# A transposing maximum that writes f16, and two small transpositions as f16 products, in a fused attention and expert layer

## The chip, the cores and the metric

The kernel runs on one core of one Trainium2 chip. The metric is device time in microseconds (us), the median of a few executions, lower is better.

## What is computed

A batch of 16 sequences of 1024 tokens, 256 wide, goes through two sublayers, each as `x = x + layernorm(f(layernorm(x)))`. The first is attention with 16 heads of 16 and relative positions:

```python
qk = einsum('bhld,bhrd->bhlr', q, k) / sqrt(16)
qk = qk + einsum('bhld,lrd->bhlr', q, rel)      # rel[l, r] = rel_emb[r - l + 511]
att = softmax(qk, axis=-1)
out = einsum('bhlr,bhrd->bhld', att, v)
```

The second is a dense product plus a shared and six routed low-rank experts, of which each token takes two.

## The kernel before

The work is 128 tiles (`NT`) of 128 queries. A tile is 16 groups (`NG`), numbered g; g = 4*jp + k, where jp is one of four pairs of 128-key chunks and k one of four sets of 32 queries (`IW`). So there are 2048 groups. Each group's scores lie in two PSUM banks (one for each chunk c of the pair) as keys on the rows and (head, query) on the columns, 16 x 32 = 512 columns a bank; three such pairs of banks (`NBUF`) go round.

For the softmax a maximum over the 256 keys of the pair is subtracted from each (head, query). Keys lie on the rows, so it is found in steps. On VectorE, `maxima` (L957) transposes 32 x 32 blocks and reduces over 32 keys: L960 writes `r1`, 128 rows x 32 columns, of which 16 belong to each chunk. On TensorE, `transpose_max` (L669) brings both halves of `r1` with two transpositions (L672) to 16 rows (heads) x 256 columns in the PSUM tile `p_max`. On VectorE, `spread` (L963) takes the maximum over the eight blocks with the sign turned (L969), writes it as f16 to `nm` (16 heads x 2 x 128 queries), and multiplies it with a mask into `nmm` (L972). On TensorE, `shift` (L681) adds `nmm` to the scores with 16 products whose stationary operand `pick` is 128 x 128 f16. Then ScalarE takes the exponential (L845), and in the next four groups TensorE multiplies `prob` with the values (L691, 32 columns of the array for each head, four heads side by side), and ScalarE copies the result out. At k=1 the product of L725 transposes the `nm` of the pair before to 128 queries x 16 heads, from which the parts of the four pairs are later rescaled against one another.

The order is written out by hand for every engine. TensorE does in group g: the scores of chunk 0 (L660 x8, 64 columns, and L665 x16, 32 columns, both with 96 rows), `transpose_max` of group g-1 (behind a wait for its maximum), the scores of chunk 1 (again L660 and L665), then `wide` and `mixed`, and at the end `shift` of group g-1. `wide` holds at k=1 and k=2 the value products L691, at k=3 four transpositions L698, at k=0 parts of the projection of a later tile (L703, L712). `mixed` holds L725 at k=1 and, in certain groups, products of the output projection and the second sublayer (L703, L712, L747). Ahead of `mixed`, and at k=2 and k=3 of `wide` as well, TensorE waits for L969 of group g-1. VectorE does in group g: `spread` of g-1, `maxima` of g, and then the `side` work of that group for layer norms, gates and rescaling (`dm` at g=1, `gate` and `ceq` at g=5, `yn` at g=13, `y2n` at g=14 among them). GpSimd masks the queries into `qm` and `rm` (L532, L533), splits f32 values into two f16 parts and does sums in f32 (`wp`, `osum`, `qkb`). In a tile it does, behind the statistics of g=13, the sum into `x1`, the masks of the next tile, and from there on the splits of that tile's start.

The unit matrices are `ident` (128 x 128, f32) and `ident16` (16 x 16, f16); GpSimd makes them once ahead of the loops.

Of the kernel before, what the change touches and what calls it, by code (L numbers as in the profile page):

```python
# [9 lines left out]
H, HD = 16, 16  # L10
# [3 lines left out]
P = 128  # L14
# [4 lines left out]
IW = 32  # L19
# [19 lines left out]
def sandwich_kernel(nc, x, wqT, bq, wkT, bk, wvT, bv, woT, bo, relT, baseT, base_b,  # L39
                    shAT, shBT, roAT, roBT, rtT, rtb, out):  # L40
    f32, f16 = mybir.dt.float32, mybir.dt.float16
    ALU = mybir.AluOpType
# [10 lines left out]
    with ctx:  # L53
        def sb(name, shape, dt=f32):
            return ctx.enter_context(nc.sbuf_tensor(name, shape, dt))
# [3 lines left out]


        ident = sb("ident", [P, P])
        ident16 = sb("ident16", [H, H], f16)
        pick = sb("pick", [P, H // 2, P], f16)
        mask_h = sb("mask_h", [H, 2, IW], f16)
        mask_q = sb("mask_q", [ROWS, H, IW], f16)
# [34 lines left out]
        qm = sb("qm", [ROWS, NI, H, IW], f16)  # L100
        rm = sb("rm", [ROWS, NI, IW // 2, H, 2], f16)
        prob = sb("prob", [P, 2, 2, H, P])
        r1 = sb("r1", [P, 2 * H])
        nm = sb("nm", [H, 2, P], f16)
        nmm = sb("nmm", [P, 2, IW], f16)
        ot = sb("ot", [P, 4, P])
        parts = sb("parts", [P, NJP, H, 17])
# [77 lines left out]
        p_max = pm[0:H, 0:2 * P]  # L185
        p_n = pm[:, 2 * P:3 * P]
# [303 lines left out]
        def _(pool):  # L490
            g = nc.gpsimd
# [9 lines left out]
            g.memset(one[:, :], 1.0)  # L501
            g.memset(vpad[:, :, :], 1.0)
            g.memset(nmm[:, :, :], 0.0)
            pool.drain()

            def keep(v, op, base, pattern, mult):
                g.affine_select(out=v, in_=v, compare_op=op, fill=0.0, base=base, pattern=pattern,
                                channel_multiplier=mult)

            keep(ident[:, :], ALU.is_equal, 0, [[-1, P]], 1)  # L510
            keep(ident16[:, :], ALU.is_equal, 0, [[-1, H]], 1)
            half_h = H // 2
            for h0 in (0, half_h):
                g.affine_select(out=pick[:, :, :], in_=pick[:, :, :], compare_op=ALU.not_equal, fill=1.0,
# [132 lines left out]
        def _(pe):  # L647
            mm = nc.tensor.matmul
# [20 lines left out]
            def transpose_max(g_count):  # L669
                pe.wait_ge(s_rmax, g_count)  # L670
                for c in range(2):
                    last = nc.tensor.transpose(p_max[:, c * P:(c + 1) * P], r1[:, c * H:(c + 1) * H], ident[:, :])  # L672
                last.then_inc(s_maxT, 1)

            def shift(buf, g_count):
# [25 lines left out]
            def transpose2(dst, src):  # L701
                for c in range(2):
                    last = nc.tensor.transpose(dst[:, c * P:(c + 1) * P], src[:, c * P:(c + 1) * P],  # L703
                                               ident[:, :])
                return last

            def product(dst, *pairs):


                steps = [(lhs(i), rhs(j)) for lhs, rhs in pairs for i, j in ((0, 0), (0, 1), (1, 0))]  # L710
                for m, (lhs, rhs) in enumerate(steps):
                    last = mm(dst, lhs, rhs, start=(m == 0), stop=(m == len(steps) - 1))  # L712
                return last

            def both(lhs, rhs, cols=slice(None)):

                return [(lambda i, c=c: lhs[:, i, c, cols], lambda j, c=c: rhs[:, j, c, :]) for c in range(2)]

            def mixed(t, g, att, a, b):


                jp, k = divmod(g, NI)
                if k == 1 and (a if jp == 0 else att):

                    mm(p_n[:, 0:H], nm[:, (jp - 1) % 2, :], ident16[:, :], start=True, stop=True)\  # L725
                        .then_inc(s_nmtp, 1)
                    return s_nmt, t * NJP + jp
                if g == 0 and b:
                    pe.wait_ge(s_xn1, t - 1)
                    transpose2(p_t, xn1).then_inc(s_x1Tp, 1)  # L730
                    return s_x1T, t - 1
                if g == 3 and b:

                    pe.wait_ge(s_x1T2, t - 1)
                    product(p_t[:, 0:NH], *both(x1T2, w_a2)).then_inc(s_hp, 1)
                    return s_hf, t - 1
                if g == 8 and a:
                    pe.wait_ge(s_o, t)
                    transpose2(p_t, o[:, :, :].rearrange("p h d -> p (h d)")).then_inc(s_oTp, 1)
                    return s_oT, t  # L740
                if g == 11 and a:
                    pe.wait_ge(s_oT2, t)
                    product(p_t, *both(oT2, w_o2)).then_inc(s_wo, 1)
                    return s_y0, t
                if g == 10 and b:
                    pe.wait_ge(s_hw, t - 1)
                    nc.tensor.transpose(p_n[0:NA, :], hw[:, :], ident[:, :]).then_inc(s_hTp, 1)  # L747
                    return s_hT, t - 1
                if g == 12 and b:
                    pe.wait_ge(s_hT2, t - 1)  # L750
                    product(p_t, *both(x1T2, w_base2), (lambda i: hT2[:, i, :], lambda j: w_b2[:, j, :]))\
                        .then_inc(s_y2p, 1)
                    return s_y20, t - 1
                return None
# [39 lines left out]
            def tile(t, n, att, proj, a, b, ph=None):  # L794
                read = None
                for g in range(NG):
                    jp, k = divmod(g, NI)
                    old = a if g == 0 else att
                    if att:
                        if k == 0:  # L800
                            pe.wait_ge(s_tw[jp], t * 16 + 16)
                            pe.wait_ge(s_ks[jp], batch_of(t) * 96 + 96)
                        if jp == 0:
                            pe.wait_ge(s_mask, t * NI + k + 1)
                        free = t * NG + g - NBUF + 1
                        if not (isinstance(free, int) and free <= 0):
                            pe.wait_ge(s_exp, free)
                        scores(g, 0, buffer(ph, g))
                    if read is not None:
                        pe.wait_ge(*read)  # L810
                    if old:
                        transpose_max(t * NG + g)
                    if att:
                        scores(g, 1, buffer(ph, g)).then_inc(s_scores, 1)

                    wide_first = k == 1 or g in (0, 8)
                    if wide_first:
                        wide(t, n, g, att, proj, a)
                    if old:
                        pe.wait_ge(s_nmr, t * NG + g)  # L820
                    read = mixed(t, g, att, a, b)
                    if not wide_first:
                        wide(t, n, g, att, proj, a)
                    if old:
                        shift(buffer(ph, g - 1), t * NG + g)
# [92 lines left out]
        def _(dve):  # L918
# [44 lines left out]
            def spread(g, count):  # L963


                jp, i = divmod(g, NI)
                dve.wait_ge(s_maxT, count)
                part = nm[:, jp % 2, i * IW:(i + 1) * IW]
                v.tensor_reduce(part, p_max.rearrange("h (q i) -> h i q", i=IW), axis=AX.X, op=ALU.max,  # L969
                                negate=True).then_inc(s_nmr, 1)  # L970
                dve.drain()  # L971
                v.tensor_tensor(nmm[0:H, :, :], part.rearrange("h (a i) -> h a i", a=1)  # L972
                                .to_broadcast((H, 2, IW)), mask_h[:, :, :], ALU.mult).then_inc(s_nm, 1)
# [90 lines left out]
            def tile(t, n, att, proj, a, b, ph=None):  # L1064
                for g in range(NG):

                    if a if g == 0 else att:
                        spread((g - 1) % NG, t * NG + g)
                    if att:
                        maxima(buffer(ph, g), t * NG + g + 1)  # L1070
                    side(g, t, n, proj, a, b)
# [35 lines left out]
```

## Time and profile before

| | us |
|---|---|
| median of 3 runs | 6519.43 (6518.75 to 6520.47) |
| profiled execution, its own time | 6501.09 |
| its span | 6499.3 |
| TensorE products busy | 6203.9 (95%) |
| VectorE busy | 5036.1 (77%) |
| GpSimd busy | 3640.9 (56%) |
| ScalarE busy | 3134.0 (48%) |

The granted clock of TensorE over the span is 0.99 of full speed, 2.4 GHz. PE are products of TensorE, PEld its weight loads, which run beside products; DVE is VectorE, ACT ScalarE, POOL GpSimd, SP the engine that issues the transfers. In a row, `128*16` after the operands are the rows and columns of the stationary operand, and then stand the shapes of the moving operand's reading or the output. A product lasts longer than the distance to the next one, since products overlap: distances are to be read from starts. A row `x16` on the timeline starts with its first instruction and ends with its last. "Idle before" is the engine's pause before the row, and behind it who ended it.

### The profile page before, as it was taken

How to read it: one execution, taken by the hardware profiler on the slowest of the kernel's cores; microseconds unless marked ns; L12 is line 12 of the kernel's file. 1: busy time of each engine (PE TensorE's matmuls, PEld its weight loads, DVE VectorE, ACT ScalarE, POOL GpSimd, SP SyncE). 2: the span in 40 equal slices, each digit the busy share in tenths (PEclk: the TensorE clock that was granted, in tenths of full speed). 3: DMA queues.
4: the chain of work that ended last, by engine and by line, in shares of the span. 5: the costliest groups of instructions: out<-in, count | busy, mean ns of one | idle time of the engine just before them, and what ended most of it. 6: DMA issues, size and time to landing. Idle time of an engine off the chain costs nothing.

```text
span 6499.3 us, 408509 instructions
## 1 busy us (share of the span) xinstructions
PE 6203.9 (95%) x178176; PEld 5783.0 (89%) x178176; DVE 5036.1 (77%) x10289; ACT 3134.0 (48%) x5145; POOL 3640.9 (56%) x4707
## 2 busy tenths in 40 slices
PE   5999999999999999999999999999999999999997
PEld 4999899999999999999999999899999999998997
DVE  3777777777787777777777777777777777777776
ACT  2444444444444444444444444444444444444444
POOL 5555555555565555555555555555555555555555
PEclk8999999999999999999999999999999999999998
DMA  3111121111212112121111211112111121211210
GB/s 86 37 44 50 37 58 37 51 45 35 58 36 59 35 35 61 35 60 33 42 56 35 60 36 48 45 39 58 35 52 43 35 58 38 59 35 33 62 35 27
DMA packets 570089, 296.73 MB, mean 46 GB/s; under 512 B 384176, under 2 KB 534688, under 8 KB 568624
## 3 DMA queue, kind: packets, MB, share of 16 engines
q1 hardware_dynamic: 568624, 272.86, 15.2%
q8 instruction: 1450, 23.76, 1.5%
q14 instruction: 15, 0.12, 0.0%
HBM read 184.46 MB, written 88.60 MB: 42 GB/s over the span
## 4 chain that ended last, share of the span: by engine, by line
PE 75%; DVE 15%; issue 6%; DVEq 3%; POOLq 1%; POOL 0%; SPq 0%; ACT 0%; DMA 0%
PE sc L665 19%; PE sc L681 13%; PE sc L660 11%; PE pw L691 11%; DVE r L960 6%; PE pm L672 6%; PE pm L712 4%; PE pw L698 4%; PE pw L712 4%; DVE nm L969 3%; DVE ceq L1008 2%; DVEq L971 2%; DVE y2n L926 1%; DVE dm L983 1%; PE pm L703 1%
## 5 line engine op out<-in xcount | busy, mean ns | idle before, releaser
L960 DVE TRANSPOSE_TENSOR_REDUCE r<-sc 128x32 f32<-128x1024 f32 x2048 | 2547.5, 1244 | 49.2 <-PE sc L665 48.3
L665 PE MATMUL sc<-rm,tw 96*128 96x32 f16 x65536 | 2288.9, 176 | 58.1 <-issue 58.1
L845 ACT ACTIVATE prob<-sc 128x1024 f32<-128x1024 f32 x2048 | 2095.7, 1023 | 237.9 <-PE sc L681 173.7
L665 PEld LDWEIGHTS sc<-rm,tw 96*128 96x128 f16 x65536 | 1976.9, 97 | 64.7 <-issue 64.3
L660 PE MATMUL sc<-qm,ks 96*128 96x64 f16 x32768 | 1635.2, 193 | 29.9 <-DMA ks<-qk_s 15.1
L969 DVE TENSOR_REDUCE nm<-pm 16x32 f16<-16x256 f32 x2048 | 840.5, 410 | 932.2 <-PE pm L672 931.4
L660 PEld LDWEIGHTS sc<-qm,ks 96*128 96x128 f16 x32768 | 1380.8, 98 | 105.7 <-issue 35.2
L681 PE MATMUL sc<-nmm,pick 128*128 128x64 f16 x32768 | 1305.7, 194 | 1.4 <-DVE nmm L972 1.4
L681 PEld LDWEIGHTS sc<-nmm,pick 128*128 128x128 f16 x32768 | 1150.9, 98 | 126.9 <-issue 103.2
L691 PE MATMUL pw<-prob,vs 128*32 128x128 f32 x32768 | 1110.2, 276 | 100.2 <-DVE nm L969 89.9
L691 PEld LDWEIGHTS pw<-prob,vs 128*32 128x32 f32 x32768 | 835.2, 110 | 158.5 <-DVE nm L969 119.8
L972 DVE TENSOR_TENSOR nmm<-nm,mask_h 16x64 f16<-16x64 f16 x2048 | 697.5, 341 | 195.0 <-issue 9.8
L672 PE MATMUL pm<-ident,r 128*16 128x128 f32 x4096 | 777.8, 271 | 0.6 <-DVE r L960 0.5
L837 ACT ACTIVATE ot<-pw 128x512 f32<-128x512 f32 x512 | 305.7, 597 | 741.4 <-PE pw L691 741.4
L545 POOL TENSOR_TENSOR oT<-oT,one 128x256 f16<-128x256 f32 x128 | 78.3, 612 | 967.4 <-ACT oT L837 967.4
L533 POOL TENSOR_TENSOR rm<-raw,mask_r 96x512 f16<-96x512 f16 x515 | 607.5, 1180 | 0.0
L532 POOL TENSOR_TENSOR qm<-raw,mask_q 96x512 f16<-96x512 f16 x515 | 590.1, 1146 | 20.7 <-PE sc L665 11.2
L837 ACT ACTIVATE nmt<-pm 128x16 f32<-128x16 f32 x512 | 94.0, 184 | 800.3 <-PE pm L725 800.3
L578 POOL TENSOR_TENSOR wp<-parts,wst 128x1088 f32<-128x1088 f32 x128 | 275.5, 2152 | 166.5 <-ACT parts L837 166.5
L837 ACT ACTIVATE parts<-pw 128x272 f32<-128x272 f32 x512 | 203.3, 397 | 315.5 <-PE pw L698 308.7
L698 PE MATMUL pw<-ident,ot 128*128 128x128 f32 x2048 | 322.9, 280 | 14.3 <-DVE nm L969 6.6
L541 POOL TENSOR_TENSOR rs<-ve,mhalf 128x1 f32<-128x1 f32 x521 | 286.3, 550 | 74.0
(129 smaller groups left out, 5753.9 us busy)
## 6 DMA issues: line engine op xcount, KB each, us to landing
raw<-qk_s SPq DMA_DIRECT2D x774, 64.0 KB, 2.5
tw<-tw_s SPq DMA_DIRECT2D x512, 72.0 KB, 2.0
v_s<-vpad SPq DMA_DIRECT2D x136, 256.0 KB, 3.4
vs<-v_s SPq DMA_DIRECT2D x64, 512.0 KB, 3.7
ks<-qk_s SPq DMA_DIRECT2D x384, 64.0 KB, 2.4
xin<-x SPq DMA_DIRECT2D x138, 128.0 KB, 2.1
qk_s<-qkh SPq DMA_DIRECT2D x272, 64.0 KB, 1.7
qk_s<-qkl SPq DMA_DIRECT2D x272, 64.0 KB, 1.6
```

Source lines behind the costliest of these rows:

```text
L532: g.tensor_tensor(qm[:, i, :, :], src, mask_q[:, :, :], ALU.mult)
L533: g.tensor_tensor(rm[:, i, :, :, :].rearrange("p i h s -> p h i s"), src.rearrange("p h (i s) -> p h i s", s=2), mask_r[:, :, :].rearrange ...
L660: last = mm(bank[:, 2 * h * IW:(2 * h + 2) * IW], ks[:, h, j:j + P], qm[:, i, 2 * h:2 * h + 2, :].rearrange("p h i -> p (h i)"), start=(h ...
L665: last = mm(out3[:, :, 2 * k:2 * k + 2], tw[:, jp, u:u + P], rm[:, i, k, :, :], start=False, stop=False, skip_group_check=True)
L672: last = nc.tensor.transpose(p_max[:, c * P:(c + 1) * P], r1[:, c * H:(c + 1) * H], ident[:, :])
L681: last = mm(pairs[:, :, h, :], pick[:, h, :], nmm[:, :, :], start=False, stop=True, skip_group_check=True)
L691: last = mm(pw[32 * q:32 * q + 32, col * P:(col + 1) * P], vs[:, 2 * jp + c, h, :], prob[:, jp % 2, c, h, :], start=(c == 0), stop=(c == 1))
L837: return A(dst, src, ACT.Copy)
L845: A(prob[:, jp % 2, :, :, i * IW:(i + 1) * IW], sc[:, 2 * buf:2 * buf + 2, :].rearrange("p c (h i) -> p c h i", i=IW), ACT.Exp).then_inc(s ...
L960: v.tensor_reduce(r1[:, :], sc[:, 2 * buf:2 * buf + 2, :].rearrange("p c (h i) -> p (c h) i", i=IW), axis=AX.X, op=ALU.max, apply_transpos ...
L969: v.tensor_reduce(part, p_max.rearrange("h (q i) -> h i q", i=IW), axis=AX.X, op=ALU.max, negate=True).then_inc(s_nmr, 1)
L972: v.tensor_tensor(nmm[0:H, :, :], part.rearrange("h (a i) -> h a i", a=1) .to_broadcast((H, 2, IW)), mask_h[:, :, :], ALU.mult).then_inc(s ...
```

## The change

`r1` becomes f16, so L960 writes its maxima as f16. The two transpositions of L672 become ordinary products of `r1` (f16, 128 x 16) with `ident16` (f16, now 128 x 128). `nm` gets 128 rows; rows 16 to 127 are set to zero once and stay so, and VectorE writes rows 0 to 15 as before. The product of L725 reads all 128 rows of `nm` and 16 columns of `ident16`.

```diff
-        ident16 = sb("ident16", [H, H], f16)
+        ident16 = sb("ident16", [P, P], f16)
...
-        r1 = sb("r1", [P, 2 * H])
-        nm = sb("nm", [H, 2, P], f16)
+        r1 = sb("r1", [P, 2 * H], f16)
+        nm = sb("nm", [P, 2, P], f16)
...
             g.memset(nmm[:, :, :], 0.0)
+            g.memset(nm[:, :, :], 0.0)
             pool.drain()
...
-            keep(ident16[:, :], ALU.is_equal, 0, [[-1, H]], 1)
+            keep(ident16[:, :], ALU.is_equal, 0, [[-1, P]], 1)
...
                 for c in range(2):
-                    last = nc.tensor.transpose(p_max[:, c * P:(c + 1) * P], r1[:, c * H:(c + 1) * H], ident[:, :])
+                    last = mm(p_max[:, c * P:(c + 1) * P], r1[:, c * H:(c + 1) * H], ident16[:, :], start=True, stop=True)
                 last.then_inc(s_maxT, 1)
...
-                    mm(p_n[:, 0:H], nm[:, (jp - 1) % 2, :], ident16[:, :], start=True, stop=True)\
+                    mm(p_n[:, 0:H], nm[:, (jp - 1) % 2, :], ident16[:, 0:H], start=True, stop=True)\
                         .then_inc(s_nmtp, 1)
...
-                part = nm[:, jp % 2, i * IW:(i + 1) * IW]
+                part = nm[0:H, jp % 2, i * IW:(i + 1) * IW]
```

## Rows read from the trace of the kernel before

**Rows 1.** The page of the kernel before: engines (part 1) and the chain (part 4).

```profile
PE 6203.9 (95%) x178176; PEld 5783.0 (89%) x178176; DVE 5036.1 (77%) x10289; ACT 3134.0 (48%) x5145; POOL 3640.9 (56%) x4707
...
PE 75%; DVE 15%; issue 6%; DVEq 3%; POOLq 1%; POOL 0%; SPq 0%; ACT 0%; DMA 0%
```

**Rows 2.** Waits of all engines: who waited for whom: us in total, times, longest.

```profile
DVE nm L969 <- PE pm L672: 931.4, 1551, 1.8
...
PEld pw L691 <- DVE nm L969: 119.8, 210, 0.8
...
PEld pw L698 <- DVE nm L969: 26.6, 126, 0.3
```

**Rows 3.** Groups by form, columns as in the page's part 5.

```profile
L960 DVE TRANSPOSE_TENSOR_REDUCE r<-sc 128x32 f32<-128x1024 f32 x2048 | 2547.5, 1244 | 49.2 <-PE sc L665 48.3 <-issue 0.3
...
L672 PE MATMUL pm<-ident,r 128*16 128x128 f32 x4096 | 777.8, 271 | 0.6 <-DVE r L960 0.5
...
L712 PE MATMUL pw<-xT,w_q 128*128 128x128 f16 x1632 | 119.7, 225 | 30.3 <-POOL xT L547 29.1 <-DVE nm L969 1.2
...
L725 PE MATMUL pm<-ident,nm 16*128 16x16 f16 x512 | 91.0, 178 | 0.0
```

**Rows 4.** Timeline of PE in one group: start us, us, what, count, idle before.

```profile
3055.85 0.56 PE L665 MATMUL sc<-rm,tw 96*128 96x32 f16 x16
3056.25 0.38 PE L672 MATMUL pm<-ident,r 128*16 128x128 f32 x2
3056.47 0.40 PE L660 MATMUL sc<-qm,ks 96*128 96x64 f16 x8
```

**Rows 5.** Timeline of PE, then of its weight loads, around L691 and L725.

```profile
3062.01 0.56 PE L665 MATMUL sc<-rm,tw 96*128 96x32 f16 x16
3062.50 1.08 PE L691 MATMUL pw<-prob,vs 128*32 128x128 f32 x32
3063.51 0.18 PE L725 MATMUL pm<-ident,nm 16*128 16x16 f16 x1
3063.62 0.64 PE L681 MATMUL sc<-nmm,pick 128*128 128x64 f16 x16
...
3063.51 0.09 PEld L725 LDWEIGHTS pm<-ident,nm 16*128 16x128 f16 x1 [0.20 <-issue]
3063.62 0.52 PEld L681 LDWEIGHTS sc<-nmm,pick 128*128 128x128 f16 x16
```

**Rows 6.** Timeline of PE: the two sets of twelve f16 products in g=4.

```profile
3095.59 0.84 PE L712 MATMUL pw<-xT,w_q 128*128 128x128 f16 x12
3096.27 0.83 PE L712 MATMUL pw<-xT,w_k 128*128 128x128 f16 x12
```

**Rows 7.** Timeline of all engines from g=5 to g=6 of one tile.

```profile
3098.78 1.04 POOL L592 TENSOR_TENSOR qkb<-qkf,b_qk 128x512 f32<-128x512 f32 x1
3098.97 0.89 DVE L972 TENSOR_TENSOR nmm<-nm,mask_h 16x64 f16<-16x64 f16 x1
...
3101.45 1.00 DVE L1008 TENSOR_TENSOR ceq<-gate 128x36 f32<-128x36 f32 x1
...
3102.93 0.54 PE L691 MATMUL pw<-prob,vs 128*32 128x128 f32 x12 [0.70 <-DVE nm L969]
```

**Rows 8.** Timeline of all engines around g=15 and around g=2 of the next tile.

```profile
3080.43 0.69 DVE L926 TENSOR_SCALAR y2n<-y,mv,rs 128x256 f32<-128x256 f32 x1
...
3081.50 0.66 PE L698 MATMUL pw<-ident,ot 128*128 128x128 f32 x4 [0.17 <-DVE nm L969]
...
3088.20 1.15 POOL L533 TENSOR_TENSOR rm<-raw,mask_r 96x512 f16<-96x512 f16 x1
...
3088.55 0.88 DVE L983 TENSOR_TENSOR dm<-nmin,nmt 128x64 f32<-128x64 f32 x1
...
3089.15 0.56 PE L665 MATMUL sc<-rm,tw 96*128 96x32 f16 x16
...
3089.82 0.43 PE L691 MATMUL pw<-prob,vs 128*32 128x128 f32 x8
```

## The prediction

> **What bounds the kernel now.** I read the engine table and the chain first, then the waits, then single groups of 32 queries on the timeline. TensorE is busy 95% of the span and holds 75% of the chain that ended last, VectorE 15% [rows 1]. The waits say where that 15% is: VectorE waits for the transpositions of L672 in 1551 of 2048 groups, so it usually has time left; the other way round, TensorE waits for `nm` (L969) about 210 times before the value products of L691 and 126 times before L698 [rows 2]. With 128 tiles of 16 groups that is three groups of a tile, and the timeline shows which: g=6 and g=15 of every tile and g=2 of most [rows 7, 8]. Everywhere else a nanosecond of TensorE is a nanosecond of the kernel.
>
> **Part 1: two f32 transpositions become two f16 products.** On the timeline one group runs L660 x8, L665 x16, L672 x2, L660 x8 with no idle time. From the start of L665 to the next L660 is 0.62 us; fifteen of the sixteen L665 steps take 15 x 25 ns = 0.375 us (0.40 us for 16), so from the last L665 to the L660 behind the transpositions is 0.245 us: 25 ns, then 110 ns for each transposition [rows 4]. An f16 product with 128 moving columns takes 0.68 us / 12 = 56 ns [rows 6]. Taken alone, that saves 54 ns twice, 0.11 us a group.
>
> But the row has a second property. The stationary operand of L672 is 128*16, and the new L672 is an ordinary product with it. Two ordinary products of the kernel use a part of the array, L691 (128*32) and L725 (16*128), and both pay when they begin and end [rows 5]: L665 to L691 is 0.49 us where L665 to L672 is 0.40, so entering costs 0.085 us (0.11 from the last L665 instead of 0.025); L725, with 16 moving columns, holds the next product back 0.11 us where the L681 behind it go 0.48/16 = 30 ns apart; and the weight loads of L725 and L681 begin in the same hundredth as their products, with 0.20 us of idle loader before L725: they are not pulled ahead. The f32 transposition of today, also 128*16, shows none of this: it comes 25 ns behind L665 and L660 comes 110 ns behind it, just its own length [rows 4]. So the row allows two readings: the narrow operand is placed on the whole array only because it is a transposition, or 16 columns never narrow the array. I take the first: L725, with only 16 rows, is an ordinary product and behaves as a narrowed one, and so does L691, with 32 columns; the new L672 is of their kind, and its 16 columns are not padded.
>
> The price under that reading: 0.11 to enter, 0.056 between the two, and to leave 0.11 (L725's) plus 112 more columns at 56/128 ns, about 0.155. Sum 0.32 us against 0.245: **0.075 us a group more, not 0.11 less.** Bounds for the leaving: 0.11 (L725 as it stands), giving +0.03, and 0.22 (the last round of L691, L691's block of 1.01 us being eight rounds), giving +0.14. I take 0.155 because the width of the moving operand is the one difference to L725. The end of the second product comes 0.11+0.056+0.225 = 0.39 us after the last L665, against 0.025+0.11+0.27 = 0.405 [rows 3, 4], so `spread` on VectorE starts practically as now; only the second half of the scores, and with it the next maxima, starts later.
>
> The Trainium skill bears on this in TensorEngine Tiling, Key Properties: changing the tiling mode drains TensorE; its Restrictions say column tiling rules out the f32 transpose mode. The first agrees with L691 and L725, the second with the absence of any gap at today's L672. Against that, the same skill's TensorE: Matmul & The Clock Gate, section "Wait — 56ns, not 53.3ns?", gives 56 ns between f16 products of 128 columns; by that alone the group would save 0.11 us, which is the first rival.
>
> **Part 2: `nm` padded to 128 rows.** L725 then takes the whole array, as L681 behind it. What it still pays is the change from L691, which L681 pays in its place at k=2. Behind it L681 follows after 25 to 30 ns instead of 110: 0.085 us less, 512 times. The lower bound is nothing (if the 0.11 were the product itself), the upper 0.085. The second memset and the larger unit matrix cost fractions of a microsecond once, ahead of the loop. VectorE writes rows 0 to 15 as before.
>
> **Part 3: the maximum writes f16.** L960 reads 1024 f32 a row from PSUM in 1244 ns and writes 32 values [rows 3]; 16-bit output of so few values I cost at nothing; no row shows this form. Bounds: 30 ns either way (the spread between its 1.23 and 1.25 us pieces doubled). It lies on the path only in three groups of a tile, so at most 3 x 128 x 0.03 = 12 us.
>
> **What is absorbed.** In front of g=6, TensorE waits 0.70 us for a stretch that VectorE and GpSimd set: `nmm` of g=5 takes 0.89 us instead of 0.18, ending with GpSimd's `qkb` (98.78+1.04), then the maxima, then `ceq` 1.00 us [rows 7]. GpSimd's run up to `qkb` started with the parts of g=3. So what TensorE loses or gains in g=4, 5 and 6, and L725 of g=5, disappears in that wait. Likewise `y2n` of g=14 (0.69 us) sets g=15, where TensorE waits 0.17, and `dm` (0.88), which ends with GpSimd's `rm` (88.20+1.15), sets g=2: there L665 to L691 is 0.67 us instead of 0.49, 0.18 us of waiting [rows 8]. In the code GpSimd writes all masks behind the statistics of g=13 in one row, so I take its run from there to g=2 as fixed, and g=14, 15, 0, 1, 2 together with L725 of g=13 and g=1 cost 5 x 0.075 - 2 x 0.085 = 0.2 us, less than the 0.35 us of waits. There remain eight groups (3 and 7 to 13) and L725 of g=9: 8 x 0.075 - 0.085 = 0.515 us a tile, x 128 = **66 us more**. The profiled execution took 6501.1 us, its span 6499.3, so it would be 6567; the median of the runs shown is 18 us above the profiled one, and 6519.4 + 66 = **6585 us**. With nothing absorbed it is 2048 x 0.075 - 512 x 0.085 = 110 us, 6630; with leaving at its lower bound, 8 x 0.03 - 0.085 = 0.155 us a tile, 6539.
>
> **Rivals.**
> First, faster: no change of the array's shape, the product goes at 56 ns. Each group then saves 0.11 and the same eight groups and one L725 count, the waits of g=2, 6 and 15 growing by what is lost: 8 x 0.11 + 0.085 = 0.965 us a tile, 123 us, 6396 us. For it: today's L672 is 128*16 and pays nothing. Against it: L725 is just as small and pays. It decides if L660 follows the second product within 0.06 us. It could give more: `nmm` of g=5 reaches VectorE only 0.19 us after `qkb` has begun [rows 7], and 0.2 us earlier it would slip in ahead of it, taking most of the 0.70 us wait with it. With every group and all L725 counted, 16 x 0.11 + 4 x 0.085 = 2.1 us a tile, it is 269 us, 6250 us.
>
> Second, no change: leaving costs as little as L725's 0.11 and more of it is absorbed in the waits than I count, or the saved 0.085 at L725 counts in all four groups: 8 x 0.03 - 4 x 0.085 is -0.1 us a tile, 13 us less, 6506 us.
>
> Third, slower than I say: leaving at 0.22, nothing absorbed, 2048 x 0.14 - 43 = 244 us, 6763 us. L691's rounds are f32 and run at half the f16 rate, so I give this little.
>
> That the f16 maximum is something other than the f32 maximum rounded is not visible in a time; `nm` is f16 already.
>
> **How the numbers follow.** The forecast has 0.70, the first rival 0.20, the second 0.08, the third 0.02. The forecast's own range is 6535 to 6640. One case in five is faster, and leaving it all out would leave no room for anything else, so the range goes down to that rival's nearer end: 6395 to 6640. About 0.2%, 13 us, is what a measurement of this kernel can tell from no change. Slower by more than that: the forecast but for its lowest edge, and the third, 0.70; same, 0.09; faster, 0.21.
>
> **What would show it.** Under the forecast L672 (f16, two products) has a mean near 225 ns, but the L665 ahead of it and the L660 behind it are 0.32 us apart, and a loader row of L672 and of L660 shows idle time or starts with its product, as L725's does now; TensorE's busy time falls while the span grows; the 0.70 us before L691 in g=6 shrinks to about 0.5. L725 to L681 is 30 ns. VectorE's total wait for L672 changes little. I am wrong if L660 starts within 60 ns of the second L672: then the first rival holds and the waits on `nm` grow. I am wrong about the absorption if the waits before L691 and L698 are as long as now. I am wrong about part 2 if L681 still comes 110 ns behind L725.

## The result and the profile after

The changed kernel takes 6637.26 us (median of 4 runs, 6616.80 to 6639.35) against 6519.56 us, 1.0173 times the kernel before, 95% interval 1.0153 to 1.0194: slower. The medians differ by 118 us; 1.0173 is 113 us, since one of the four runs is 20 us faster than the others and counts fully in the ratio. The profiled execution took 6616.8 us, 116 us more than that of before. The diff adds lines, so L672 is now L673, L660 and L665 are L661 and L666, L691 is L692, L698 is L699, L712 is L713, L725 is L726, and L969 is L970.

First the page: span, engines, and the chain.

```profile
span 6615.0 us, 408510 instructions
...
PE 6310.2 (95%) x178176; PEld 5679.0 (86%) x178176; DVE 5147.6 (78%) x10289; ACT 3137.3 (47%) x5145; POOL 3639.0 (55%) x4708
...
PE 86%; DVE 7%; issue 5%; DVEq 1%; POOLq 1%; POOL 0%; SPq 0%; ACT 0%; DMA 0%
PE sc L666 22%; PE sc L661 16%; PE pw L692 15%; PE sc L682 14%; PE pm L673 6%; PE pw L713 4%; PE pm L713 3%; PE pw L699 3%; DVE xn L927 3%; DVE r L961 2%; PE pm L704 1%; PE pm L726 1%; DVEq L972 1%; DVE nm L970 1%; DVE ceq L1009 1%
```

Against [rows 1], products are busy for 106 us more, although each L673 got shorter, and the chain has moved from VectorE (15% to 7%) to TensorE (75% to 86%). Then one group on TensorE's timeline (start, length in us, what, count), and the weight loads of the same stretch:

```profile
3066.24 0.56 PE L666 MATMUL sc<-rm,tw 96*128 96x32 f16 x16
3066.73 0.28 PE L673 MATMUL pm<-ident,r 128*16 128x128 f16 x2
3066.94 0.41 PE L661 MATMUL sc<-qm,ks 96*128 96x64 f16 x8
```

```profile
3066.73 0.10 PEld L673 LDWEIGHTS pm<-ident,r 128*16 128x16 f16 x2
3066.94 0.29 PEld L661 LDWEIGHTS sc<-qm,ks 96*128 96x128 f16 x8
```

From L666 to L673 is 0.49 us, where it was 0.40 in [rows 4]: 0.115 us from the last L666 instead of 0.025. From L673 to the next L661 is 0.21. The weight loads of L673 and of L661 start with their own products, as L725's did in [rows 5]: they aren't pulled ahead. Taken from the starts in all groups, the median distances are 106 ns into the first product, 60 between the two and 152 out of the second, 318 ns together; before they were 25, 108 and 108, 241 ns. I read that as the array emptied twice a group; the experiments below test it. Now L726:

```profile
3103.73 1.08 PE L692 MATMUL pw<-prob,vs 128*32 128x128 f32 x32
...
3104.74 0.10 PEld L726 LDWEIGHTS pm<-ident,nm 128*128 128x128 f16 x1 [0.20 <-issue]
3104.75 0.18 PE L726 MATMUL pm<-ident,nm 128*128 128x16 f16 x1
...
3104.78 0.63 PE L682 MATMUL sc<-nmm,pick 128*128 128x64 f16 x16
```

L682 begins 0.03 us behind L726 (39 ns by the median, 110 before), so the padding of `nm` does what the prediction said. (L726's own row below is at 183 ns; what TensorE is held is the distance.) And the costliest groups by form (busy us, mean ns of one, idle before), with the waits on `nm`:

```profile
L961 DVE TRANSPOSE_TENSOR_REDUCE r<-sc 128x32 f16<-128x1024 f32 x2048 | 2551.3, 1246 | 102.6 <-PE sc L666 55.6
...
L661 PE MATMUL sc<-qm,ks 96*128 96x64 f16 x32768 | 1658.6, 194 | 30.5 <-DMA ks<-qk_s 15.6 <-issue 14.9
...
L673 PE MATMUL pm<-ident,r 128*16 128x128 f16 x4096 | 572.6, 222 | 0.5 <-DVE r L961 0.5
...
L927 DVE TENSOR_SCALAR xn<-xin,mv,rs 128x256 f32<-128x256 f32 x137 | 216.8, 1583 | 37.1 <-POOL rs L542 37.1
...
L726 PE MATMUL pm<-ident,nm 128*128 128x16 f16 x512 | 93.7, 183 | 0.0
```

```profile
PE pw L713 <- DVE nm L970: 92.4, 88, 1.1
...
PE pw L692 <- DVE nm L970: 24.8, 39, 0.6
```

L961 takes 1246 ns against 1244 [rows 3]: the f16 write of the maxima is free. L673 has fallen from 271 to 222 ns. Two rows are new. The normalisation of `xin` into `xn`, a VectorE instruction of group 3 that took 387 ns in the mean, takes 1583. And TensorE waits 88 times, 92 us in all, for `nm` in front of the `w_q` products of group 4, where it had waited 1.2 us in all (it stands behind L712 in [rows 3]). In return the waits before the value products have shrunk from 89.9 to 24.8 us. The timeline of two tiles shows what `xn` does; first one where it is held, then one where it isn't:

```profile
3046.62 2.25 DVE L927 TENSOR_SCALAR xn<-xin,mv,rs 128x256 f32<-128x256 f32 x1
...
3046.69 2.04 POOL L579 TENSOR_TENSOR wp<-parts,wst 128x1088 f32<-128x1088 f32 x1 [1.01 <-ACT parts L838]
...
3049.26 0.84 PE L713 MATMUL pw<-xT,w_q 128*128 128x128 f16 x12 [1.05 <-DVE nm L970]
```

```profile
3148.06 0.37 DVE L927 TENSOR_SCALAR xn<-xin,mv,rs 128x256 f32<-128x256 f32 x1
...
3148.13 2.20 POOL L579 TENSOR_TENSOR wp<-parts,wst 128x1088 f32<-128x1088 f32 x1 [1.02 <-ACT parts L838]
...
3149.50 0.83 PE L713 MATMUL pw<-xT,w_q 128*128 128x128 f16 x12
```

In both `xn` starts 0.07 us ahead of GpSimd's `wp`. In the first it ends only after `wp` has (46.69 + 2.04), and TensorE waits 1.05 us; in the second it takes 0.37 us and it is `wp` that takes 2.20 instead of 2.04. In the kernel before, `xn` started 0.11 us ahead of `wp` in 126 tiles and was held in none of them; there too the two overlap, and it is `wp` that is lengthened, to 2.15 us. (In one tile `xn` started 0.10 us behind `wp` and took 2.08 us.)

Where `xn` isn't held, `ceq` of group 5 is: it takes about 1 us in the 39 tiles whose `xn` took 0.37 us, and 0.2 us in the tiles whose `xn` was held. So a tile that has waited for `nm` in group 4 doesn't wait for it again in group 6.

### The profile page after: what moved, and what is told of

It is laid out like the page before. It is cut to its first block, busy times and chain, and to the rows that moved or that the text cites. A ratio compares the mean times of both kernels' runs of the same rounds, so it can differ in the third digit from the quotient of the medians.

```text
span 6615.0 us, 408510 instructions
## 1 busy us (share of the span) xinstructions
PE 6310.2 (95%) x178176; PEld 5679.0 (86%) x178176; DVE 5147.6 (78%) x10289; ACT 3137.3 (47%) x5145; POOL 3639.0 (55%) x4708
## 4 chain that ended last, share of the span: by engine, by line
PE 86%; DVE 7%; issue 5%; DVEq 1%; POOLq 1%; POOL 0%; SPq 0%; ACT 0%; DMA 0%
PE sc L666 22%; PE sc L661 16%; PE pw L692 15%; PE sc L682 14%; PE pm L673 6%; PE pw L713 4%; PE pm L713 3%; PE pw L699 3%; DVE xn L927 3%; DVE r L961 2%; PE pm L704 1%; PE pm L726 1%; DVEq L972 1%; DVE nm L970 1%; DVE ceq L1009 1%
## 5 line engine op out<-in xcount | busy, mean ns | idle before, releaser
L961 DVE TRANSPOSE_TENSOR_REDUCE r<-sc 128x32 f16<-128x1024 f32 x2048 | 2551.3, 1246 | 102.6 <-PE sc L666 55.6
L666 PE MATMUL sc<-rm,tw 96*128 96x32 f16 x65536 | 2288.9, 176 | 56.4 <-issue 56.3
L666 PEld LDWEIGHTS sc<-rm,tw 96*128 96x128 f16 x65536 | 1978.2, 97 | 62.1 <-issue 61.8
L661 PE MATMUL sc<-qm,ks 96*128 96x64 f16 x32768 | 1658.6, 194 | 30.5 <-DMA ks<-qk_s 15.6
L970 DVE TENSOR_REDUCE nm<-pm 16x32 f16<-16x256 f32 x2048 | 839.6, 410 | 847.4 <-PE pm L673 846.7
L661 PEld LDWEIGHTS sc<-qm,ks 96*128 96x128 f16 x32768 | 1220.0, 98 | 267.1 <-issue 40.4
L682 PE MATMUL sc<-nmm,pick 128*128 128x64 f16 x32768 | 1302.8, 193 | 3.2 <-issue 2.0
L682 PEld LDWEIGHTS sc<-nmm,pick 128*128 128x128 f16 x32768 | 1159.7, 98 | 119.0 <-issue 105.7
L692 PE MATMUL pw<-prob,vs 128*32 128x128 f32 x32768 | 1111.5, 276 | 26.9 <-DVE nm L970 24.8
L692 PEld LDWEIGHTS pw<-prob,vs 128*32 128x32 f32 x32768 | 835.2, 110 | 73.9 <-DVE nm L970 28.7
L973 DVE TENSOR_TENSOR nmm<-nm,mask_h 16x64 f16<-16x64 f16 x2048 | 650.5, 318 | 195.2 <-issue 9.8
L673 PE MATMUL pm<-ident,r 128*16 128x128 f16 x4096 | 572.6, 222 | 0.5 <-DVE r L961 0.5
L699 PE MATMUL pw<-ident,ot 128*128 128x128 f32 x2048 | 320.4, 279 | 4.5 <-ACT ot L838 0.3
```

The costliest lines, as they stand in the source:

```text
L661: last = mm(bank[:, 2 * h * IW:(2 * h + 2) * IW], ks[:, h, j:j + P], qm[:, i, 2 * h:2 * h + 2, :].rearrange("p h i -> p (h i)"), start=(h ...
L666: last = mm(out3[:, :, 2 * k:2 * k + 2], tw[:, jp, u:u + P], rm[:, i, k, :, :], start=False, stop=False, skip_group_check=True)
L673: last = mm(p_max[:, c * P:(c + 1) * P], r1[:, c * H:(c + 1) * H], ident16[:, :], start=True, stop=True)
L682: last = mm(pairs[:, :, h, :], pick[:, h, :], nmm[:, :, :], start=False, stop=True, skip_group_check=True)
L692: last = mm(pw[32 * q:32 * q + 32, col * P:(col + 1) * P], vs[:, 2 * jp + c, h, :], prob[:, jp % 2, c, h, :], start=(c == 0), stop=(c == 1))
L961: v.tensor_reduce(r1[:, :], sc[:, 2 * buf:2 * buf + 2, :].rearrange("p c (h i) -> p (c h) i", i=IW), axis=AX.X, op=ALU.max, apply_transpos ...
```

## The experiments

Two theories were open. **The shape:** the products use a part of the array only, because their stationary operand has 16 columns and they are no f32 transposition. **The collision:** the new `xn` wait has a price of its own, beside the shape. The rivals were that f16 (the write of the maxima, the product) costs the time, and that the shape alone makes up the 118 us. The ratios below are to the kernel before, run on the same chip at the same time, with the 95% interval.

### The products on the whole array

```diff
-        r1 = sb("r1", [P, 2 * H], f16)
+        r1 = sb("r1", [P, H + P], f16)
...
+            g.memset(r1[:, :], 0.0)
...
-                    last = mm(p_max[:, c * P:(c + 1) * P], r1[:, c * H:(c + 1) * H], ident16[:, :], start=True, stop=True)
+                    last = mm(pm[:, c * P:(c + 1) * P], r1[:, c * H:c * H + P], ident16[:, :], start=True, stop=True)
...
-                v.tensor_reduce(r1[:, :], ...
+                v.tensor_reduce(r1[:, 0:2 * H], ...
```

> The change, with one part undone: r1 is 144 columns wide, zero beyond 32, and each product takes 128 of its columns as the stationary operand instead of 16, so it uses the whole array. Theory (the narrow stationary operand empties the array on both sides): the last L666 to the first transposing product falls from 106 to 25 ns, the next score product follows within 60 ns instead of 152, the three distances together from 318 to about 140 ns. If every group counts, 2048 x 0.178 = 365 us below the changed kernel, about 6270; with VectorE's waits taking part of it, 6270 to 6400. Rival (the f16 write of the maxima or the f16 product itself is slow): no distance changes, 6600 or more.

Measured: 6332.78 us, 0.9733 (0.9717 to 0.9750). The same group on the timeline:

```profile
3096.46 0.56 PE L667 MATMUL sc<-rm,tw 96*128 96x32 f16 x16
3096.86 0.27 PE L674 MATMUL pm<-ident,r 128*128 128x128 f16 x2
3096.97 0.40 PE L662 MATMUL sc<-qm,ks 96*128 96x64 f16 x8
```

L667 to L674 is 0.40 us and L674 to L662 is 0.11; the median distances are 25, 55 and 55 ns, 135 together. So 112 more columns in the stationary operand (zeros, but for 16 of the first product's, whose output isn't read) cost nothing and give back 183 ns a group, 375 us if all of it counted; against the changed kernel's 1.0173 the gain is 4.4 per cent, some 286 us. The f16 write and the f16 products are still there, so they aren't what costs the time. The rest of the 375 us went into waits, as [rows 2] had them but longer:

```profile
PE pw L693 <- DVE nm L971: 123.8, 125, 1.0
...
PE pw L700 <- DVE nm L971: 53.9, 127, 0.5
```

This version beats both kernels. One surprise is in its VectorE rows:

```profile
L928 DVE TENSOR_SCALAR xn<-xin,mv,rs 128x256 f32<-128x256 f32 x137 | 52.2, 381 | 36.7 <-POOL rs L543 36.7
...
L985 DVE TENSOR_TENSOR dm<-nmin,nmt 128x64 f32<-128x64 f32 x128 | 34.3, 268 | 9.6
...
L1010 DVE TENSOR_TENSOR ceq<-gate 128x36 f32<-128x36 f32 x128 | 26.0, 203 | 9.6
L1011 DVE TENSOR_TENSOR cgt<-gate 128x36 f32<-128x36 f32 x128 | 145.8, 1139 | 0.0
```

`ceq` takes 203 ns here and took 1.0 us in [rows 7]; `dm` takes 268 and took 0.88 in [rows 8]. For `ceq` nothing is gained by it: the instruction behind it, `cgt`, takes 1139 ns where it took 191, so the delay of group 5 has only moved on by one instruction. The shorter groups shift VectorE's instructions against GpSimd's, and another one is held. `xn` itself shows that its lead over `wp` doesn't decide alone: here it starts only 0.03 to 0.04 us ahead of `wp` in 76 tiles and 0.11 in 50, and isn't held in any of them; `wp` takes 2.20 us in the mean.

### A stationary operand of 64 columns

The same edit with 64 in place of P, and rows 0 to 63 of `pm` as the output.

> The stationary operand padded to 64 columns instead of 128, otherwise as the padded kernel. Theory (any part of the array's columns is another shape): the same 106, 60 and 152 ns as with 16 columns, time as the changed kernel, 1.01 to 1.02 of the kernel before, xn meeting wp in some tiles. Rival (only quarters of 32 columns cost): 25, 56 and 56 ns, 0.973.

Measured: 6630.02 us, 1.0187 (1.0170 to 1.0204).

```profile
L674 PE MATMUL pm<-ident,r 128*64 128x128 f16 x4096 | 615.0, 232 | 0.5 <-DVE r L962 0.5
...
L928 DVE TENSOR_SCALAR xn<-xin,mv,rs 128x256 f32<-128x256 f32 x137 | 171.9, 1255 | 36.5 <-POOL rs L543 36.5
```

Median distances 106, 80 and 152 ns. Half the columns are as bad as an eighth of them; between the two products it is even 20 ns more.

### Without f16: an ordinary f32 product

```diff
-        r1 = sb("r1", [P, 2 * H], f16)
+        r1 = sb("r1", [P, 2 * H])
...
-                    last = mm(..., r1[:, c * H:(c + 1) * H], ident16[:, :], start=True, stop=True)
+                    last = mm(..., r1[:, c * H:(c + 1) * H], ident[:, :], start=True, stop=True)
```

> r1 stays f32 and L673 is an ordinary f32 product of the same 128 x 16 operand instead of a transposition. Theory (an ordinary product narrows the array whatever its type; only the f32 transposition does not): 106 ns into the first, about 205 out of the last as behind L692, the block from the last L666 to L661 0.40 us or more against 0.24 in the kernel before; at 8 to 16 groups a tile 1.02 to 1.05 of the kernel before. Rival (the narrow use comes with f16): 25 ns into it, and the block 0.24 to 0.45 us only through the length of f32 products.

Measured: 7437.01 us, 1.142 (1.1401 to 1.144), far more than expected.

```profile
3000.46 0.56 PE L666 MATMUL sc<-rm,tw 96*128 96x32 f16 x16
3000.95 0.61 PE L673 MATMUL pm<-ident,r 128*16 128x128 f32 x4
3001.49 0.41 PE L661 MATMUL sc<-qm,ks 96*128 96x64 f16 x8
```

The entry is the same 106 ns, the exit 205 as behind L691. What I had missed is the count: the trace has four L673 for the two products, 120, 109 and 109 ns apart. Each ordinary f32 product has two rows in the trace, where the f32 transposition has one. The kernel before showed it already: `pv` makes 16 f32 products a group, and L691 stands with x32 in [rows 5]. The block is 106 + 338 + 205 = 0.65 us against 0.24; 2048 x 0.41 = 840 us, most of the 928 measured. The shape theory holds (the same 128*16 f32 operand as before, and only the transposition is gone); its price was off by a factor of 2.6 (0.41 us a group more instead of 0.16), and f16 as the cause of the narrow use is refuted.

### As an f16 transposition

```diff
-        p_max = pm[0:H, 0:2 * P]
+        p_max = pm[0:H, 0:P].bitcast(f16)
...
-                    last = mm(p_max[:, c * P:(c + 1) * P], r1[:, c * H:(c + 1) * H], ident16[:, :], start=True, stop=True)
+                    last = nc.tensor.transpose(p_max[:, c * P:(c + 1) * P], r1[:, c * H:(c + 1) * H], ident16[:, :])
```

> The changed kernel with both f16 products as f16 transpositions of the same 128 x 16 operand, into an f16 view of the same PSUM tile, which VectorE's L970 then reads as f16. Theory A (it is the f32 transposition alone that keeps the whole array, as the page says for f32 only): 106, 60 and 152 ns, 1.01 to 1.02 of the kernel before. Theory B (any transposition keeps it): 25, 56 and 56 ns, and the time of the padded kernel, 0.973.

Measured: 6619.10 us, 1.0160 (1.0141 to 1.0178), with 106, 59 and 152 ns.

```profile
L970 DVE TENSOR_REDUCE nm<-pm 16x32 f16<-16x256 f16 x2048 | 838.5, 409 | 838.3 <-PE pm L673 837.1
...
L673 PE MATMUL pm<-ident,r 128*16 128x128 f16 x4096 | 572.3, 222 | 0.4 <-DVE r L961 0.3
```

Theory A. An f16 transposition of this operand is placed like an f16 product; it is the f32 transposition that keeps the whole array. The Trainium skill, TensorEngine Tiling (Array Packing), Gotcha 2: Feature Incompatibilities, lists the transpose mode as excluded by column tiling for f32 input only. The traces agree with it: with the 128*16 operand only the f32 transposition has 25 ns in front of it and 108 behind; the f16 transposition, the f16 product and the f32 product have 106 in front and 152 or 205 behind. Here `xn` is held in 121 tiles, though the three distances are those of the changed kernel.

### The padding of nm alone

The changed kernel with `r1` back at f32 and L673 an f32 transposition.

> Only the padding of nm to 128 rows: r1 stays f32 and L673 an f32 transposition. L726 to L682 falls from 110 to 39 ns, 512 times. The prediction counted it in one group of four: 128 x 0.071 = 9 us less than the kernel before, 6510. Rival (it counts in all four, nothing is absorbed): 36 us less, 6483.

Measured: 6496.07 us, 0.9985 (0.9976 to 0.9995): 10 us less, against 9 expected. L726 to L682 is 39 ns, so 36 us were there to be had (42 with L682's second product, which follows the first in 28 ns instead of 39); the waits say who took them:

```profile
PE pw L692 <- DVE nm L970: 112.6, 207, 0.8
...
PEld pw L699 <- DVE nm L970: 37.9, 126, 0.4
```

TensorE now waits 207 times and 112.6 us before the value products, where it was 89.9 us, and the loader waits longer before L699 too, 37.9 us against 26.6 [rows 2].

### The products alone

The changed kernel with `nm` and its unit matrix at 16 rows.

> The changed kernel without the padding of nm: r1 and both products as changed, nm and its unit matrix with 16 rows. Theory: L726 to L682 back at 110 ns, between 9 us (the absorption that the padding alone met on the kernel before) and 36 us (all four groups count) above the changed kernel, 1.018 to 1.023 of the kernel before; the three distances round L673 stay 106, 60 and 152. The number of tiles in which xn meets wp may move, 0.35 to 0.5 us each. Rival (padding nm is what adds time, through 128 rows of weights in L726): faster than the changed kernel.

Measured: 6643.53 us, 1.0205 (1.0188 to 1.0222). Again 88 waits before L713, and L726 to L682 at 111 ns. Against 1.0173 the missing padding costs some 21 us, between the two bounds given; the intervals of the two ratios overlap, so the size is rough.

### xn away from wp, in the changed kernel

```diff
-                if g == 3 and proj:
+                if g == 10 and proj:
                     dve.wait_ge(s_rs0, n + 2)
                     dve.wait_ge(s_xTp, n + 1)
                     normal(xn[:, :], xin[:, :], mv0, rs0).then_inc(s_xn, 1)
```

> The changed kernel, with VectorE's normalisation of xin into xn moved from group 3 to group 10, away from GpSimd's wp. Theory (in 88 of 128 tiles xn begins 70 ns before wp and is held 1.9 us by it, about 1.05 us of it on the path): 90 to 110 us less than the changed kernel, 6525 to 6550, and xn at 0.37 to 0.39 us everywhere. Rival (the 118 us are the array's emptying alone, 2048 x 0.077 - 512 x 0.071 = 121 us, and the collision lies beside the path): 6615 to 6640 as before the move.

Measured: 6573.78 us, 1.0105 (1.0088 to 1.0122). The form's row, and the waits:

```profile
L927 DVE TENSOR_SCALAR xn<-xin,mv,rs 128x256 f32<-128x256 f32 x137 | 60.9, 444 | 37.2 <-POOL rs L542 37.2
...
L1004 DVE TENSOR_SCALAR gate<-eg,rg 128x6 f32<-128x6 f32 x128 | 153.9, 1202 | 9.9
```

```profile
PEld pw L692 <- DVE nm L970: 98.8, 126, 0.8
...
PE pw L692 <- DVE nm L970: 86.2, 126, 0.7
...
PEld pw L699 <- DVE nm L970: 7.0, 41, 0.2
```

The direction is the collision theory's: 0.68 per cent, 44 us, are gone. The size isn't: I expected 90 to 110, and `xn` at 0.37 to 0.39 us, where it is 0.44. The wait in group 4 was 92 us, but without it the wait in group 6 is back, 86.2 us instead of 24.8, and in group 5 it is now `gate` that is held, 1202 ns against 242 in the kernel before. So a collision of `xn` costs 44/88 = 0.5 us a tile, half of what the row of the wait says.

### The same move in the kernel before

> The same move in the kernel before, where xn never met wp (0.37 us in every tile). Theory: no difference, 6510 to 6530. Rival (the place at group 10 is better or worse by itself, by letting maxima of group 4 start elsewhere): more than 13 us either way, and the effect in the changed kernel would have to be read less this.

Measured: 6503.23 us, 0.9994 (0.9985 to 1.0004). The place of `xn` has no price to be seen where `xn` isn't held. The wait in group 6 is shorter by it, though: 76.6 us in 126 tiles, where it was 89.9.

### A collision made in the kernel before

```diff
                     dve.wait_ge(s_xTp, n + 1)
+                    v.tensor_copy(nudge[:, 0:1], mhalf[:, :])
+                    v.tensor_copy(nudge[:, 1:2], mhalf[:, :])
                     normal(xn[:, :], xin[:, :], mv0, rs0).then_inc(s_xn, 1)
```

> The kernel before, with two copies of one column put in front of xn in group 3 on VectorE, so that xn comes some 0.15 us later. It begins 113 ns ahead of wp in the kernel before. Theory (xn that begins after, or less than about 70 ns ahead of, wp is held by it for 1.9 us): xn at 1.9 to 2.3 us in nearly every tile, TensorE waiting about 1 us on nm in group 4 and correspondingly less in group 6, in sum 0.4 to 0.6 us a tile, 50 to 80 us, ratio 1.008 to 1.012. Rival (the long xn is a consequence of the narrow products and has no price of its own): xn stays at 0.37 us or costs nothing, 0.998 to 1.002.

Measured: 6567.26 us, 1.0083 (1.0065 to 1.0101).

```profile
L927 DVE TENSOR_SCALAR xn<-xin,mv,rs 128x256 f32<-128x256 f32 x137 | 284.7, 2078 | 0.0
```

```profile
PE pw L713 <- DVE nm L970: 144.0, 127, 1.2
```

Two copies of one column, 0.11 and 0.14 us, on an engine with a quarter of its time free, cost 54 us by the ratio (58 by the medians): `xn` now starts 0.025 us ahead of `wp`, is held in all 127 tiles, and TensorE waits 127 times in group 4. That is 54/127 = 0.43 us a tile, near the 0.5 from the other side. No product is touched here, so the collision has its own price. What the copies cost where they cause no collision was not run; a wait of 1.1 us in group 4 is more than their length.

### Both mends together

The products on the whole array, and `xn` in group 10.

> Both: the products on the whole array (stationary operand padded to 128 columns) and xn in group 10. In the padded kernel the waits on nm before L693 and L700 are 124 and 54 us, and none stands at xn. Theory (xn costs time only where it meets wp, which it doesn't there): as the padded kernel alone, ratio 0.973, within 0.002. Rival (the place in group 3 holds up VectorE anyway): 0.965 or less.

Measured: 6357.89 us, 0.9765 (0.9749 to 0.9782), against 0.9733 without the move. Neither theory expected it to be slower, and it seems so by about 0.3 per cent (the two intervals just meet). One row has changed back:

```profile
L1010 DVE TENSOR_TENSOR ceq<-gate 128x36 f32<-128x36 f32 x128 | 124.8, 975 | 9.5
```

`ceq` is at 975 ns again, 203 without the move, but that isn't the 0.3 per cent: `cgt` is short again in its place (182 ns), and from the L674 of group 6 to that of group 7 the tile takes 0.06 us less than without the move. The time is lost between groups 13 and 2, 0.29 us a tile; why is open.

## Why the prediction came out as it did

**The shape of the array: right.** The step that decided the sign, that an ordinary product with a 128*16 operand is narrowed while the f32 transposition isn't, came from comparing L672 with L691 and L725, and the padded, the 64-column, the f32 and the f16-transposed versions confirm it. Of the three terms, entering was predicted at 0.11 and measured at 0.106, the distance between at 0.056 and measured at 0.060, leaving at 0.155 and measured at 0.152. Their sum was 0.32 against 0.245 and is 0.318 against 0.241: 0.077 us a group, 158 us over 2048 groups, where 0.075 was predicted. The first rival, 56 ns and no change of shape, is refuted for 16 and for 64 columns, and is exactly what the padded version does.

**L725: right** as to the distance (0.071 us instead of 0.085), and the padding alone brought 10 us where the prediction counted the one group of four that isn't absorbed.

**The maximum in f16: right,** 2 ns.

**The sum: the term that failed is the absorption,** "There remain eight groups (3 and 7 to 13)", with nothing counted for the other eight. It gave 66 us; measured were 118 by the medians. The traces say where: the time from the first L672 or L673 of a group to that of the next, as the mean of tiles 5 to 119, against the kernel before, in ns a tile:

| groups | predicted | changed kernel | with `xn` in group 10 |
|---|---|---|---|
| 3 and 7 to 13 | 515 | 280 | 283 |
| 4 to 6 | 0 | 396 | 95 |
| 14, 15, 0, 1, 2 | 0 | 219 | 199 |
| tile | 515 | 895 | 577 |

Three things are in it. First, the collision of `xn` with `wp`, which the prediction didn't look at: it checked what VectorE's delayed instructions already waited for and not what they would newly meet. It is the difference of the last two columns, 0.3 us a tile in groups 4 to 6, about 40 us.

Second, the groups that were to be absorbed weren't. The wait before g=6, which was to fall to about 0.5 us, is 86.2/126 = 0.68 us with `xn` out of the way, against 89.9/126 = 0.71 before, and 0.61 in the kernel before with the same move. The prediction took GpSimd's run up to `qkb` as setting this wait whatever TensorE does; it hardly shrank, so that step was wrong, and what sets the wait in its place wasn't tested. At g=15 and g=2 waits did go (the loader waits 41 times before L699 against 126, and 126 times before L692 against 210 [rows 2]), but the five groups around them still take 0.2 us a tile more.

Third, the groups that were to count in full gave only half. The block round L673 costs 77 ns more, and the first L661 step behind it 7 ns more (39 instead of 32; all L661 steps together 867 us instead of 844, a loss that the prediction left out); groups 8 and 14 show the whole of it, 85 ns. In groups 9 and 13 L725 takes off the same again, as predicted. But in groups 3, 7, 10, 11 and 12 (and 4) the first product behind the second half's scores starts 25 ns after the last L666, where it took 54 to 58, and 35 to 40 ns a group are left. In the padded version that step is 54 to 58 as before. No wait is in it, and why it is shorter beside the narrow products is open.

So the 68 us of the version with `xn` moved (1.0105 of 6506), which look like the predicted 66, are luck: half of them come from groups that were counted at nothing, and the groups counted gave 283 ns instead of 515.

**The edges.** The median lies 3 us inside the forecast's own range of 6535 to 6640. The prediction's 6630 for "nothing absorbed" is near the measured time for a wrong reason: part was made good elsewhere, and the collision put it back.

**Left open:** what decides whether `xn` or `wp` is held. In the changed kernel `xn` starts 0.07 us ahead of `wp` both in 87 of the 88 tiles where it is held and in the 39 where it isn't; 0.025 us ahead it was always held in the nudged kernel, and 0.03 to 0.04 us ahead never in the padded one. The number of held tiles differs between versions with the same distances in front of and behind L673: 88 in the changed kernel, 88 without the padding of `nm`, 121 with the f16 transpositions. The four runs of the changed kernel differ by 22 us, the spread of some 45 collisions at 0.5 us; that the number also differs from run to run is an inference, since the other three have no trace here.

## What to carry to other kernels

Before a small f32 transposition is turned into an f16 product, look at the columns of its stationary operand: with fewer than the whole array's, the product empties the array on both sides, 0.16 us a pair here, more than the faster type gives back; zeros up to 128 columns cost no time on TensorE and turned +1.7 into -2.7 per cent. When a change delays one engine by tenths of a microsecond, list what the delayed instructions will newly run into on the other engines, not only what they wait for today; here a normalising VectorE instruction that came to start 0.07 instead of 0.11 us ahead of a long GpSimd one was held in two tiles of three, worth 44 us. A start ahead of the other is no safety margin: 0.035 us ahead it was never held in another version. And when such an instruction gets short again, look at its neighbours before you book the gain: the delay of `ceq` turned up in `cgt` or `gate`. A wait's row is an upper bound of its price: here the next wait down the line took back half of it. A total that fits isn't a mechanism that fits: 68 us against 66 came from the wrong groups.

## What was not expected of the hardware

An ordinary f32 product has two rows in the trace (four L673 for two, 8192 where the others have 4096, and 32 L691 for 16), while an f32 transposition is one of 108 ns. VectorE's `tensor_scalar` on f32 and GpSimd's `tensor_tensor` held each other up for the whole length of the one that got there first: 2.25 us for an instruction of 0.37, which ends 0.15 us behind `wp`. The one that loses isn't always the one that started later by the trace: `xn` started 0.07 us first in 87 of the 88 tiles where it lost. Beside the narrow products a following whole-array product starts 25 ns behind the last score product instead of 54 to 58. Two products with 64 stationary columns follow each other in 80 ns, with 16 or 128 columns in 60 and 55; ahead of them all, 25 ns turn into 106 for 16 and for 64 columns.
